# Channel attention: when the reciprocal of the row sums is taken, when a tile is finished, and three extra unit-matrix products at each turn

## The reference, cut to what matters

```
ch = width // N_HEADS
q = qkv.reshape(bs * N_HEADS, ch, length)
k = v = y.reshape(bs * N_HEADS, ch, -1)
scale = 1.0 / math.sqrt(math.sqrt(ch))
weight = jnp.einsum('bct,bcs->bts', q * scale, k * scale)
weight = jax.nn.softmax(weight.astype(jnp.float32), axis=-1)
a = jnp.einsum('bts,bcs->bct', weight, v)
...
x = x + _L1_xattn_ref(_layernorm(x, axis=-1), ctx_2048)
x = x + _L1_ffn_ref(_layernorm(x, axis=-1), ...)
```

## Time and profile before

| | |
|---|---|
| device time, median of 3 runs | 1905.09 us (1902.85 to 1906.1) |
| the profiled execution: its time | 1906.64 us |
| the profiled execution: its span | 1904.8 us |
| mean granted TensorE clock | 0.973 |
| PE busy | 1715.1 us (90%) |
| DVE busy | 1477.7 us (78%) |
| ACT busy | 1025.8 us (54%) |
| POOL busy | 718.4 us (38%) |

### The profile page before, as it was taken

How to read it: one execution, slowest core, us unless ns; L and a number is a source line. 1 busy time by engine, 2 the same in 40 slices (tenths; PEclk the granted TensorE clock), 3 DMA queues, 4 the chain that set the end, 5 groups by cost and what they waited for, 6 DMA issues and landing times.

```text
span 1904.8 us, 43494 instructions
## 1 busy us (share of the span) xinstructions
PE 1715.1 (90%) x15835; PEld 1014.5 (53%) x15896; DVE 1477.7 (78%) x2884; ACT 1025.8 (54%) x2056; POOL 718.4 (38%) x965
## 2 busy tenths in 40 slices
PE   5999999889999999979968986788778989999998
PEld 2666665556777777755544552222222456656555
DVE  5776666789989899848977889899999478666654
ACT  3656565355555555534336765788889433333222
POOL 4645321378767677512335453444531000000000
PEclk9999999999999999989988997999999999999999
DMA  9601110000000000000001212333321023222121
GB/s 257 175 24 51 30 41 2 7 18 20 15 12 11 12 5 6 2 9 1 1 1 40 58 36 60 86 94 92 98 73 44 16 84 98 76 74 67 57 84 50
DMA packets 87644, 94.62 MB, mean 50 GB/s; under 512 B 17568, under 2 KB 63264, under 8 KB 87456
## 3 DMA queue, kind: packets, MB, share of 16 engines
q1 hardware_dynamic: 83712, 87.76, 16.0%
q10 hardware_dynamic: 2976, 2.32, 0.5%
q0 software_dynamic: 768, 2.10, 0.4%
HBM read 78.51 MB, written 10.22 MB: 47 GB/s over the span
## 4 chain that ended last, share of the span: by engine, by line
PE 22%; DVE 14%; issue 6%; DMA 6%; POOL 3%; SPq 3%; ACT 1%; DVEq 0%; POOLq 0%; ACTq 0%
PE ps L292 18%; DVE arena L1655 6%; DMA ch_out<-arena 2%; POOL arena L1203 2%; SPq L1479 1%; DMA arena<-ch_inverse 1%; DMA ch_inverse<-arena 1%; PE ps L1923 1%; DMA arena<-ch_out 1%; PE ps L1616 1%; PE ps L1920 1%; DVE arena L2504 1%; DVE arena L2500 0%; DVE arena L1257 0%; DVE arena L2016 0%
## 5 line engine op out<-in xcount | busy, mean ns | idle before, releaser
L292 PE MATMUL ps<-arena 128*128 128x512 f16 (+6 forms) x6403 | 1083.5, 322 | 48.9 <-POOL arena L1203 11.1
L292 PEld LDWEIGHTS ps<-arena 128*128 128x128 f16 (+1 forms) x6464 | 601.3, 99 | 429.1 <-issue 30.4
L1641 ACT ACTIVATE arena<-ps 128x512 f32<-128x512 f32 x512 | 269.5, 597 | 73.9 <-PE ps L1565 70.5
L1655 DVE TENSOR_REDUCE arena<-ps 128x4 f32<-128x1024 f32 x256 | 292.6, 1211 | 3.7 <-PE ps L1558 3.3
L1616 PE MATMUL ps<-arena 128*32 128x256 f32 x2048 | 166.7, 399 | 0.2 <-ACT arena L1650 0.2
L2494 DVE TENSOR_TENSOR arena<-ps,arena 128x512 f32<-128x512 f32 x96 | 66.1, 688 | 127.5 <-ACT arena L2386 108.5
L1558 PE MATMUL ps<-arena 31*128 31x256 f16 x1024 | 103.7, 284 | 66.0 <-DVE arena L1655 62.0
L2386 ACT ACTIVATE arena<-ps 128x512 f32<-128x512 f32 x96 | 57.1, 596 | 179.2 <-PE ps L292 178.9
L1558 PEld LDWEIGHTS ps<-arena 31*128 31x128 f16 x1024 | 29.3, 93 | 173.7 <-DVE arena L1655 143.1
L1565 PE MATMUL ps<-arena 32*128 32x256 f16 x1024 | 117.8, 279 | 0.0
L1107 POOL TENSOR_TENSOR arena<-arena 128x512 f32<-128x512 f32 x96 | 98.7, 1042 | 46.2 <-DVE arena L232 44.8
(11 more groups left out here) (205 smaller groups left out, 2982.0 us busy)
## 6 DMA issues: line engine op xcount, KB each, us to landing
arena<-moe_cw SPq DMA_DIRECT2D x64, 192.0 KB, 2.8
arena<-moe_cw SPq DMA_DIRECT2D x64, 128.0 KB, 2.9
arena<-in_L_ffn_gate_up_proj SPq DMA_DIRECT2D x16, 384.0 KB, 3.4
ch_out<-arena SPq DMA_DIRECT2D x32, 128.0 KB
arena<-moe_cw SPq DMA_DIRECT2D x64, 64.0 KB, 2.7
ch_keys<-arena SPq DMA_DIRECT2D x48, 64.0 KB, 2.0
arena<-ch_keys SPq DMA_DIRECT2D x64, 48.0 KB
arena<-arena SPq DMA_DIRECT2D x192, 16.0 KB
```

The costliest lines, as they stand in the source:

```text
L292: last = nc.tensor.matmul(out, a, b, start=start and n == 0, stop=stop and n == len(pairs) - 1, skip_group_check=not group)
L1641: nc.scalar.activation(pT[:, b % 3, g], ps[:, T[n % len(T)], :].rearrange("p (u t) -> p u t", u=KD), ACT.Exp, scale=CH_SCALE).then_inc(s_e ...
L1655: nc.vector.tensor_reduce(m[:, half % 2, 2 * half_pair:2 * half_pair + 2, j, :], ps[:, bank(user):bank(user) + 2, :].rearrange("p g (u s) ...
```

## The change

Four things change. In VectorE's program the reciprocal moves from the turn in the middle of a tile to the turn at a tile's start, that is half a tile later, and the statistics move the other way, from the start to the middle. In SP's program `store_inverse` goes to the front of the next round, behind its first `load_max`; `load_out` brings the tile before, and stands ahead of the last three transfers of `load_q` instead of behind them. In GpSimd's program `finish` takes the tile before, so that every tile is finished one round later. And TensorE makes three products of the 128 x 128 unit matrix with itself behind each turn, into a part of a bank that nobody reads.

```
+CH_WARM = 3
...
             if 0 <= 2 * n - 1 < CH_HALVES:
                 load_max(2 * n - 1)
+            if 0 <= n - 3 < TILES:
+                store_inverse(n - 3)
             stage(2 * n - 1)
...
                 load_q(sp, n + 2, range(5, 9))
-            if 0 <= n - 2 < TILES:
-                store_inverse(n - 2)
+            if 0 <= n - 3 < TILES:
+                load_out(n - 3)
             if n + 2 < TILES:
                 load_q(sp, n + 2, range(9, CH_KEYROWS))
-            if 0 <= n - 2 < TILES:
-                load_out(n - 2)
...
             nc.tensor.transpose(ps[0:32, bank(user), 0:P], m[:, half % 2]..., core.ident).then_inc(s_scored, 1)
+            keep_warm(nc, ps[:, bank(user) + 1, 0:P], core.ident, CH_WARM)
...
-            if t % CH_SETS == CH_HALF and tile >= 2:
-                invert(dve, tile - 2)
-            if t % CH_SETS == 0 and SUBS <= tile < TILES:
+            if t % CH_SETS == 0 and tile >= 3:
+                invert(dve, tile - 3)
+            if t % CH_SETS == CH_HALF and tile >= SUBS:
                 measured(dve, tile - SUBS)
...
-            if 0 <= tile - 2 < TILES:
-                finish(pool, tile - 2)
+            if 0 <= tile - 3 < TILES:
+                finish(pool, tile - 3)
```

## The result

| | before | changed |
|---|---|---|
| time, median of 4 runs each | 1903.97 us (1901.67 to 1906.10) | 1888.98 us (1886.37 to 1891.16) |
| ratio | 1 | 0.9923 [0.9910, 0.9936] |
| profiled execution: time, span | 1906.64, 1904.8 | 1889.12, 1887.3 |
| turn 3 to turn 30 (27 halves; turns are numbered from 0) | 278.95 | 262.64 |
| last stretch: turn 30 to the first norm of the MoE (L255) | 12.55 | 12.95 |

What follows compares the result with a forecast made beforehand. The prediction took a ring of transfers through SP's queue and GpSimd to set the pace, with VectorE's waits only showing it. -18.7 + 0.55 + 1.2 = -17.0 us gave a median of 1888.1 us, range 1885 to 1894.

Steps and rivals of the forecast that it cites:

- the ring: Loop through SP's queue and GpSimd (load_v, store_out, load_total, load_out, finish, set_v): 20.19 us against 19.28 for VectorE's two halves.
- the +1.2 for tile 3: Tile 3's round: load_max, behind the MoE's constants on SP, comes late and stalls; with tile 4 +1.2 us, 0 to 3.5.
- the 9.64 us: VectorE's time from turn to turn, half a tile, whenever nothing is late in the channel attention.
- The stalls, -18.7: VectorE's 27 halves took 278.95 us, at 9.64 each 260.3; the excess of 18.7 us was to go.
- The new ring, 17.6 us with 1.7 to spare: SP's new order takes 2.56 us out of 20.19, leaving the loop 1.7 us below VectorE's 19.28.
- `load_v` waits for `set_v` and not for the queue: On SP, store_inverse (0.45 us) ahead of load_v was to be harmless for this reason.
- the ring still sets the pace in part: Rival, chance 0.12: the loop stays near 20.19 us and the wait moves to TensorE; 11 us lost, 1899.
- The landing of the 8 KB transfer: Time for load_max to land in tile 3's round, taken as 2.0 us, between rows of 2.0 and 3.4.
- The last turn, +0.55: One more reciprocal between VectorE's last negation and the MoE's norm, with no reductions to hide it: +0.55 us.
- The products, "some 0.34 us, cost nothing": Three unit-matrix products at each of 32 turns fit TensorE's 0.85 us hole; 0 to 0.6 us in all at half clock.
- each further one 0.11: Price of each added product on TensorE, from four in 0.61 us in the cross attention and one alone in 0.27.
- The rival that they lift the clock: Chance 0.05: products at the second turn bring 2.4 GHz sooner, the 1.5 us lost there come back; 1886.6 us.

Runs made afterwards that it cites:

- the exchange on GpSimd: Kernel before, with GpSimd's second set_v of a round ahead of finish instead of behind it; 1891.75 us, ratio 0.9931.

## Why the prediction was right, and what in it was mis-sized

**What bounds the kernel: shown, in three ways.** Opening the ring (the exchange on GpSimd, 262.46 us) and shortening it (the change, 262.64 and 260.77) bring nearly the same; lengthening it costs 36 us with the reciprocal in its new place.

**The stalls, -18.7: measured -16.3 in one profile and -18.2 in the other** (278.95 less 262.64 and 260.77), the +1.2 for tile 3 included, so -17.5 was predicted. Most halves take the 9.64 us.

**The new ring, 17.6 us with 1.7 to spare: mis-sized, without harm to the sum.** Its shortest round is 18.29 in this profile, and 17.95 in the one with the constants moved to tile 13, so its best rounds come near the estimate; most don't. Three things were wrong. I took 20.19 us from a single round of before, where the mean of eleven was 20.97. And I let the wait of `load_total` behind `store_out` stay at 3.90 us. In the round that begins at 1283.89 it is 4.64:

```profile
1283.11 0.42 SPq L197 DMA_DIRECT2D arena<-in_L_ffn_gate_up_proj  x1
1283.89 0.50 SPq L1485 DMA_DIRECT2D arena<-in_ctxT  x1
1284.43 0.53 SPq L1495 DMA_DIRECT2D ch_out<-arena  x1
...
1289.07 0.63 SPq L1502 DMA_DIRECT2D arena<-ch_out  x1
...
1302.38 1.99 SPq L197 DMA_DIRECT2D arena<-in_L_ffn_gate_up_proj  x1
1304.41 0.43 SPq L1485 DMA_DIRECT2D arena<-in_ctxT  x1
```

The store (128 KB) now follows 1.32 us behind a 384 KB weight load. The traces of all fourteen profiles bear this out as a pattern: where the store is issued less than 1.5 us behind the weight load, `load_total` follows it by 4.17 to 5.59 us (64 rounds, median 4.98); where it comes 3 to 7 us behind, by 3.69 to 4.35 (43 rounds, median 4.04). Of the eleven rounds named above, nine are of the second kind in the kernel before, and five are of the first in the changed one. No run moved the weight load alone, so that it is the load which lengthens the store's way is likely and not shown.

The third thing is the sentence that "`load_v` waits for `set_v` and not for the queue". At the end of the same round `set_v` was done at 1302.97, but the issue of the next weight load took 1.99 us, and `load_v` came at 1304.41; this round is 20.52 us. Such issues of over 1 us belong to the new order: in the fourteen profiles of the stage they are 23 of the 100 weight loads that stand directly behind `store_inverse`, and none of the 194 that stand elsewhere. The ring thus has a microsecond to spare in its best rounds and less than none in its worst, and the mean is 19.37. The rival "the ring still sets the pace in part" was nearer than its 0.12 says: with three transfers more it holds.

**Tile 3, +1.2 (0 to 3.5): inside its range in both profiles, at 1.2 in neither.** 2.3 us above an undisturbed half in the first profile and 0.4 in the second, where all 27 halves together are 0.6 above 260.14. Its cause is the constants' place in SP's queue, as the prediction said: the stall goes with them. The landing of the 8 KB transfer was taken as 2.0 us from a row for 64 KB; `load_max` issued at 1216.10 let the scores go on at 1217.95, so it landed in at most 1.9. The prediction's 2.0 us from the Trainium skill ("DMA: Bandwidth & Descriptors", section "Anatomy of one DMA — SWDGE (gpsimd) path") stands in a section on transfers that GpSimd issues, and this one is SP's; the trace comes close to it here. In the stalls of two other kernels the scores went on 1.80 us (constants in tile 13) and 2.44 us (`load_out` last) behind the issue of `load_max`.

**The last turn, +0.55: +0.40**, and it comes back when the reciprocal goes behind the norm.

**The products, "some 0.34 us, cost nothing": cost right, size wrong by 2.4 times.** They took 0.83 us, 0.67 of it in the hole of 0.85 between transpose and scores, so TensorE was left idle for 0.18 us and not for the about 0.5 that the prediction named as a sign. The step that failed is "each further one 0.11": I took a row for one product, where one fp32 product of this size is two rows; the four rows there are two products. The hole was nearly full, and with six products a half costs 0.42 us more and the time is that of the kernel before within its interval. At the two turns at half clock the reductions waited 0.48 us longer with them, each time: 0.96 us, where 0 to 0.6 in all was foreseen, though the time doesn't show it. The rival that they lift the clock brought no time: with and without them, the times and the stretch from turn 0 to turn 3 are alike. Its price of 1.5 us stands in no row.

**The sum** came out well with a little luck: 1.75 us of the profiled execution's gain lie ahead of the stretches that the prediction spoke of, and are scatter.

## What to carry to other kernels

An engine that waits is where a lateness shows, not where it arises: compare the time of a round on every queue with the busy time of a round on the busiest engine, over many rounds and not one, and follow the transfer that is late through the queues until it comes back to itself. Here the ring was opened most cheaply by exchanging two calls on the engine that isn't busy. Then move whatever else stands in that queue (constants, weight chunks) to a place with nothing late behind it, and price filler work by its own row, in the number of rows that one operation makes.

## What the runs showed of the hardware that was not expected

- A 128 x 128 fp32 product stands in the trace as two matmul rows: three took 0.83 us, six 1.50, at the upper clock level, and three at the lower one:

```profile
1161.39 1.49 PE L262 MATMUL ps<-arena 128*128 128x128 f32 x6
```

- Issuing one transfer on SP took between 0.42 and 1.99 us for the same kind of weight load in one profile of the changed kernel. In this in-order queue that alone moved a round of 19 us by 1.4. All issues of over 1 us stood directly behind the small store of the reciprocals (23 of 100; none of 194 elsewhere); why is open.
- The lower clock level (0.50) at the start of the stage lasted 27.3 us in five of the six profiles without products and 30.7 in the sixth; in the seven with three products it lasted 20.5 to 30.7, 23.9 or less in five of them. That the products shorten it is suggested by this, not shown, and no time comes of it: turn 0 to turn 3 took 34.52 to 35.27 us without them and 34.27 to 35.34 with. With six, the clock stood at its upper level for 3.4 us (1151.3 to 1154.7) inside the stretch at the start of the stage that is otherwise at the lower one (1144.5 to 1168.4); it didn't pay for their 0.42 us a half.
